# Attention maxima turned whole and split behind the transposes; eight decay products by GpSimd, one more bank copy by ScalarE

## The reference

```python
# mixer (a state space block, four heads of 64, chunks; here one chunk product per tile of 128 rows)
h = layernorm(x); z, xs, Bc, Cc, dt = split(h @ W_in)      # silu, softplus, rope
M = (Ck @ Bk.T)[None] * exp(segsum(dt * A))                # scores times decays, causal
y = M @ (xs * dt) + carried state + D * xs
x1 = layernorm(x + rms(y * silu(z)) @ W_out)
# cross attention, 16 heads of 8: q from x1, k and v from the context
att = softmax(q @ k.T / sqrt(8), axis=3); x2 = layernorm(x1 + (att @ v) @ Wo.T)
# feed-forward: each of 2048 rows goes to its best 2 of 8 experts (128 -> 512 -> 128)
out = layernorm(x2 + weighted sum of two experts)
```

## Time and profile before

| what | value |
|---|---|
| median of three runs | 432.17 us (431.09 to 432.71) |
| the profiled execution | 424.11 us, its span 422.8 us |
| mean granted clock of PE | 0.921 |
| PE busy | 343.0 us, 81% |
| DVE busy | 290.7 us, 69% |
| ACT busy | 236.0 us, 56% |
| POOL busy | 223.2 us, 53% |

### The profile page before, as it was taken

The page is one execution under the profiler, slowest core; times in us unless marked ns, Lnnn a source line. Parts: engine busy times, 40 slices in busy tenths (PEclk is TensorE's granted clock), DMA queues, the critical chain, the costliest instruction groups (busy, mean ns, idle before and its releaser), DMA issues.

```text
span 422.8 us, 8816 instructions
## 1 busy us (share of the span) xinstructions
PE 343.0 (81%) x2781; PEld 232.8 (55%) x2781; DVE 290.7 (69%) x829; ACT 236.0 (56%) x462; POOL 223.2 (53%) x322
## 2 busy tenths in 40 slices
PE   1999978888878788889877588788999999999600
PEld 1666655555534444444443344367879998998500
DVE  3465645888887898967895826356787667666455
ACT  1677645432666576544776558543545656656405
POOL 2670598854444453543589768926554333233426
PEclk9999999999998999977997669689999999999955
DMA  8833222626505040504435233301213211110163
GB/s 265 316 103 110 101 78 86 188 84 183 163 30 163 5 137 5 158 11 141 132 94 145 85 83 120 90 25 39 56 52 91 72 44 45 52 53 29 35 198 99
DMA packets 44156, 41.96 MB, mean 99 GB/s; under 512 B 4512, under 2 KB 38112, under 8 KB 44112
## 3 DMA queue, kind: packets, MB, share of 16 engines
q1 hardware_dynamic: 40976, 35.10, 28.1%
q0 software_dynamic: 2272, 4.69, 3.2%
q10 hardware_dynamic: 864, 1.61, 1.1%
HBM read 26.36 MB, written 14.75 MB: 97 GB/s over the span
## 4 chain that ended last, share of the span: by engine, by line
PE 52%; DVE 21%; POOL 13%; issue 8%; ACT 4%; DMA 3%; DVEq 0%; POOLq 0%; ACTq 0%
PE banks L993 12%; DVE nm L1186 8%; PE banks L1020 6%; POOL slots_dram L1679 4%; PE banks L690 4%; PE banks L1008 4%; PE banks L838 4%; PE banks L886 3%; PE banks L1021 2%; PE banks L747 2%; DVE ctx_in L1128 2%; ACT probs_all L1495 1%; PE banks L913 1%; POOL w_split L1691 1%; DMA ctx_in<-in_L_ffn_w 1%
## 5 line engine op out<-in xcount | busy, mean ns | idle before, releaser
L1186 DVE TENSOR_REDUCE nm<-banks 128x4 f32<-128x1024 f32 x64 | 78.0, 1219 | 16.9 <-PE banks L829 16.5
L1495 ACT ACTIVATE probs_all<-banks 128x1024 f32<-128x1024 f32 x64 | 65.4, 1022 | 39.3 <-PE banks L838 38.9
L1695 POOL DMA_INDIRECT y_dram<-x,scatter_u x39 | 37.5, 962 | 56.1 <-DVE x L1347 54.2
L993 PE MATMUL banks<-w_split,scores_in 128*128 x234 | 65.3, 415 | 0.0
L838 PE MATMUL banks<-scores_in 32*128 32x256 f32 x256 | 35.2, 352 | 24.6 <-DVE nm L1186 13.1
L838 PEld LDWEIGHTS banks<-scores_in 32*128 32x128 f32 x256 | 21.6, 202 | 50.9 <-DVE nm L1186 22.5
L1326 DVE TENSOR_TENSOR ctx_in<-ctx_in,banks 128x512 f32<-128x512 f32 x39 | 26.8, 688 | 28.6 <-ACT ctx_in L1542 28.3
L993 PEld LDWEIGHTS banks<-w_split,scores_in 128*128 128x128 f32 x234 | 41.5, 192 | 7.8 <-issue 0.8
L1679 POOL DMA_INDIRECT slots_dram<-rows,place_u x32 | 31.8, 995 | 26.3 <-DVE count L1286 18.9
L886 PE MATMUL banks<-probs_all,vals 128*9 128x256 f32 x512 | 45.1, 429 | 0.3
L1542 ACT ACTIVATE ctx_in<-banks 128x512 f32<-128x512 f32 x39 | 23.3, 598 | 36.6 <-PE banks L993 36.6
(11 more groups left out here) (222 smaller groups left out, 761.4 us busy)
## 6 DMA issues: line engine op xcount, KB each, us to landing
scores_in<-k_dram SPq DMA_DIRECT2D x32, 128.0 KB, 2.7
scores_in<-q_dram SPq DMA_DIRECT2D x32, 128.0 KB, 2.9
ctx_in<-in_L_ffn_w SPq DMA_DIRECT2D x16, 256.0 KB, 2.7
cs_wide<-cs_dram SPq DMA_DIRECT2D x14, 256.0 KB, 3.5
scores_in<-slots_dram SPq DMA_DIRECT2D x39, 65.0 KB, 1.9
k_dram<-split_qk SPq DMA_DIRECT2D x8, 256.0 KB, 2.5
q_dram<-split_qk SPq DMA_DIRECT2D x8, 256.0 KB, 2.3
ctx_in<-in_L_ffn_wo SPq DMA_DIRECT2D x8, 256.0 KB, 2.8
```

Of the source, the lines that this page charges most:

```text
L993: m = TE.matmul(up_bank(i, j), xT[:, i % XT, xh, :], all_weights[:, c + j * FF:][:, bass.ds(expert_at[i], FF)], start=n == 0, stop=n == 2)
L1186: V.tensor_reduce(most, maxima_of(n).rearrange("p (j k q) -> p j k q", j=2, k=TPS), AX_X, ALU.max, negate=True).then_inc(s["nmax"], 1)
L1495: C.activation(probs(n).rearrange("p j k q -> p (j k q)"), EXPS, ACT.Exp, scale=SCALE).then_inc(s["probs"], 1)
L1695: G.indirect_dma_start(y_dram[:, :], bass.IndirectOffsetOnAxis(ap=scatter_u[:, i:i + 1], axis=0), y_slot[:, i % Y_RING, :], None).then_inc ...
```

## The change

The maxima of a batch are transposed whole (16 columns instead of 32), in the same step as before. ACT writes the rounded part of the turned rows out of the bank (L1490, now 16 x 256), and in the step after, ahead of that step's scores, DVE writes the remainder, bank minus rounded part (`maxima_low`, 16 x 256). MISC is free only after this. SP then sends each of the two by a DMA of its own (`send_maxima`), also placed at the head of that step, and so behind the earlier step's `load_weights`. DVE's two instructions L1193 and L1195 and the tile `nm_parts` are gone. DVE's L1202 is done by ACT, as the second half of its `evacuate`. DVE's L1128 is done by POOL for the tiles from 8 on.

```diff
-SPLIT_LAG, ROWS_LAG = 0, 3
+ROWS_LAG = 3
+MATRIX_BY_POOL = 8
@@ middle_order
+        for b in range(B):
+            if n == PAIRS_B * (b + 1) - LEAD + ROWS_LAG:
+                yield "maxima_low", b
+                yield "send_maxima", b
         if exps is not None or maxima is not None:
             yield "scores", exps, maxima
...
-        for stage, lag in (("split_maxima", SPLIT_LAG), ("maxima_out", ROWS_LAG)):
-            b, late = divmod(n + LEAD + 1 - lag, PAIRS_B)
-            if not late and 1 <= b <= B:
-                yield stage, b - 1
+        for b in range(B):
+            if n == PAIRS_B * (b + 1) - LEAD - 1 + ROWS_LAG:
+                yield "maxima_out", b
@@ SP
-            def maxima_out(b):
+            def send_maxima(b):
                 r = b % RING
-                q.wait_ge(s["nm_out"], b + 1)
+                q.wait_ge(s["nm_lo"], b + 1)
                 q.wait_ge(s["nmax"], PAIRS_B * (b + 1))
-                SY.dma_start(queries[3:P:16, r, :, :].bitcast(F32), nm_rows[:, :].bitcast(F32)).then_inc(a[f"mr{r}"], 16)
+                for i in range(2):
+                    SY.dma_start(queries[3 + 16 * i:P:32, r, :, :].bitcast(F32),
+                                 nm_rows[:, i, :].bitcast(F32)).then_inc(a[f"mr{r}"], 16)
@@ PE
             def maxima_out(b):
-                q.wait_ge(s["nm_split"], 2 * (b + 1))
+                q.wait_ge(s["nmax"], PAIRS_B * (b + 1))
                 misc.wait()
                 for k in range(TPS):
-                    m = TE.transpose(MISC[0:2 * AH, k * P:(k + 1) * P],
-                                     nm_parts[:, k].rearrange("p j i r -> p (j i r)").bitcast(F32), ident)
+                    m = TE.transpose(MISC[0:AH, k * P:(k + 1) * P], nm[:, b % 2, k, :], ident)
                 m.then_inc(s["nm_t"], 1)
-                misc.freed_at(s["nm_out"], b + 1)
+                misc.freed_at(s["nm_lo"], b + 1)
@@ DVE
             def mix_matrix(t):
...
+                if t >= MATRIX_BY_POOL:
+                    return
...
-            def split_maxima(b):
...
-            def evacuate(b, half):
...
+            def maxima_low(b):
+                q.wait_ge(s["nm_hi"], b + 1)
+                V.tensor_tensor(nm_rows[:, 1, :], MISC[0:AH, 0:S], nm_rows[:, 0, :].bitcast(F32), ALU.subtract).then_inc(s["nm_lo"], 1)
@@ ACT
-                C.activation(nm_rows[:, :], MISC[0:2 * AH, 0:S], ACT.Identity).then_inc(s["nm_out"], 1)
+                C.activation(nm_rows[:, 0, :], MISC[0:AH, 0:S], ACT.Identity).then_inc(s["nm_hi"], 1)
...
             def evacuate(b, half):
+                q.wait_ge(s["av_mm"], GR * b + (half + 1) * GR // 2)
+                q.wait_ge(s["heads_t"], TPS * b)
+                q.wait_ge(a["init_dram"], INIT)
+                C.activation(avT[:, half * BANK:(half + 1) * BANK], AV, ACT.Identity).then_inc(s["av_hi" if half else "av_lo"], 1)
@@ POOL
+            def mix_matrix(t):
+                if t < MATRIX_BY_POOL:
+                    return
+                q.wait_ge(s["score"], GROUP)
+                q.wait_ge(s["decay"], t + 1)
+                G.tensor_tensor(decay[:, t % 3], decay[:, t % 3], scores[:, t, :].unsqueeze(1).to_broadcast([P, NH, P]),
+                                ALU.mult).then_inc(s["mat"], 1)
```

More of the change, by code:

```diff
@@ L371, in build @@
         nm = sb("nm", [P, 2, TPS, AH])
-        nm_parts = sb("nm_parts", [P, TPS, GJ, 2, GR], F32R)
-        nm_rows = sb("nm_rows", [2 * AH, S], F32R)
+        nm_rows = sb("nm_rows", [AH, 2, S], F32R)
         rec = sb("rec", [P, AH])
@@ L503, in build @@
         INIT = 16 * 3
-        MAX_ROWS = 16
+        MAX_ROWS = 16 * 2
         def sums_turned(t):
@@ L654, in sync_program @@
             stages = dict(keys_values=keys_values, query=query, load_keys=load_keys, load_queries=load_queries,
-                          maxima_out=maxima_out, load_weights=load_weights, sums=sums, load_sums=load_sums,
+                          send_maxima=send_maxima, load_weights=load_weights, sums=sums, load_sums=load_sums,
                           clear_rows=clear_rows, load_tile=load_tile)
@@ L1184, in maxima @@
                 q.wait_ge(s["max_mm"], n + 1)
-                q.wait_ge(s["nm_split"], 2 * (b - 1))
+                q.wait_ge(s["nm_t"], b - 1)
                 V.tensor_reduce(most, maxima_of(n).rearrange("p (j k q) -> p j k q", j=2, k=TPS), AX_X, ALU.max,
                                 negate=True).then_inc(s["nmax"], 1)
-            def split_maxima(b):
[L1190 to L1195, removed]
-            def evacuate(b, half):
[L1198 to L1202, removed]
+            def maxima_low(b):
+                q.wait_ge(s["nm_hi"], b + 1)
+                V.tensor_tensor(nm_rows[:, 1, :], MISC[0:AH, 0:S], nm_rows[:, 0, :].bitcast(F32), ALU.subtract).then_inc(s["nm_lo"], 1)
             def divide(b, half):
@@ L1356, in vector_program @@
             middle = dict(mix_matrix=mix_matrix, mix=mix, mix_residual=mix_residual, mix_norm=mix_norm,
-                          query=query, maxima=maxima, split_maxima=split_maxima, evacuate=evacuate,
+                          query=query, maxima=maxima, maxima_low=maxima_low,
                           divide=divide, out_project=out_project, x2_norm=x2_norm, gate_top=gate_top, choose=choose,
@@ L1498, in evacuate @@
             def evacuate(b, half):
-                if half == 0:
-                    q.wait_ge(s["av_mm"], GR * b + GR // 2)
-                    q.wait_ge(s["heads_t"], TPS * b)
-                    q.wait_ge(a["init_dram"], INIT)
-                    C.activation(avT[:, 0:BANK], AV, ACT.Identity).then_inc(s["av_lo"], 1)
+                q.wait_ge(s["av_mm"], GR * b + (half + 1) * GR // 2)
+                q.wait_ge(s["heads_t"], TPS * b)
+                q.wait_ge(a["init_dram"], INIT)
+                C.activation(avT[:, half * BANK:(half + 1) * BANK], AV, ACT.Identity).then_inc(s["av_hi" if half else "av_lo"], 1)
             def turn_heads(b):
@@ L1714, in pool_program @@
                 G.tensor_scalar(w_out[:, c, :], w_out[:, c, :], rms_w[:, c:c + 1], 0.5 * float(np.sqrt(DI)), ALU.mult, ALU.mult).then_inc(s["consts_g"], 1)
-            middle = dict(mask_decays=mask_decays, scale_inputs=scale_inputs, mix=mix, turn_mixed=turn_mixed,
+            middle = dict(mask_decays=mask_decays, mix_matrix=mix_matrix, scale_inputs=scale_inputs, mix=mix, turn_mixed=turn_mixed,
                           mix_residual=mix_residual, evacuate=evacuate, out_project=out_project, choose=choose, place_chosen=place_chosen,
```

2 lines of the change are left out of this document (1 added, 1 removed).

## The result

The changed kernel takes 438.41 us in the median (435.00 to 445.58, 4 runs), the kernel before beside it 432.10 (431.09 to 432.71): the record gives a ratio of 1.0248, 95% interval 1.0166 to 1.0331. The forecast was 428.5 (424.5 to 434.3). Two later comparisons gave 1.0137 (1.0041 to 1.0232) and 1.0124 (1.0086 to 1.0161). The 1.0248 is more than the listed times yield, whose medians give 1.0146, so I rely on the two repeats: the change costs about 1 to 1.5%, some 4 to 6 us.

What follows compares the result with a forecast made beforehand. PE and DVE alternate from 96 to 238 us, neither full; later a 4.1 us wait is on the path. Terms -4.1 -1.9 +1.2 -0.2 +0.6 -1.0 +1.7 sum to -3.7 us: 428.5 us, range 424.5 to 434.3.

Steps and rivals of the forecast that it cites:

- The stall: DVE's rounding copy L1193 of batch 7, 4.92 us beside POOL's run, holds up PE; removing it gives -4.1 us.
- no change: Rival: the stall is rarer in timed runs, or POOL's pieces absorb the gain; 432 us, chance 0.20.
- The maxima: Two small DVE instructions gone, -1.0 us; the new remainder ahead of reductions in batches 0 to 3, +1.7 us.
- The serial link: Rival: ACT's copy, DVE's remainder, then reduction and MISC's release in series; 1.43 us a late batch, 435.4 us, chance 0.15.
- Decay products: Eight of sixteen products move from DVE to POOL: -1.9 us on DVE, +1.2 us for normalisations waiting beside POOL.
- the 1.3 to 1.9 that was named: Sign of being right: two L1171 normalisations of batches 3 to 5 take between 1.3 and 1.9 us together.
- The copy: Second bank copy moves from DVE to ACT: -0.2 us on DVE, +0.6 us at step 49, where PE awaits ACT's exponentials.
- The clock: Rival: a shorter pause keeps PE at 2.4 GHz from 238 to 276 us; 3.5 us more gain, 425 us, chance 0.12.
- Stretch 96 to 238 within 1.5 us: Sign of being right: the stretch from 96 to 238 us stays within 1.5 us of its old length.

Runs made afterwards that it cites:

- c0: The kernel before, unaltered, profiled and timed again beside itself: ratio 0.9954 (0.9908 to 1.0001).
- e1: The kernel before with the maxima part only; second bank copy and all decay products stay on DVE: ratio 1.0115 (1.0036 to 1.0195) to before.
- g3: Maxima part alone, bank freed by ACT's unrounded copy, both rows made by DVE from SBUF: ratio 1.0116 (1.0052 to 1.0180) to before.
- g2: Maxima part alone, with DVE making each remainder twice: ratio 1.0226 (1.0131 to 1.0321) to before.
- f2: The kernel before with only the decay products of tiles 8 to 15 moved to POOL: ratio 0.9947 (0.9906 to 0.9988) to before.
- h4: The kernel before with only the decay products of tiles 8 to 15 on POOL, measured again: ratio 1.0023 (0.9978 to 1.0068) to before.
- e3: The changed kernel with all sixteen decay products given back to DVE: ratio 1.0188 (1.0106 to 1.0271) to before.
- f1: The kernel before with only the second bank copy moved to ACT: ratio 0.9973 (0.9937 to 1.0009) to before.
- f3: The changed kernel with ACT copying the bank unrounded and POOL making both rows, no remainder on DVE: ratio 1.0119 (1.0074 to 1.0165) to before.

## Why the prediction was wrong, step by step

- **The stall, -4.1 us: the step that failed.** It was taken as part of the kernel, from one execution in which seven of eight instances were 181 ns. Six further traces of kernels with this instruction have none. The text named this as the "no change" rival and argued against it by the fixed place of the instruction; the place was fixed and the meeting still was not. By the traces its worth is 0 in six of seven; the timed runs do not single it out.
- **The maxima, -1.0 and +1.7: mis-sized.** The part measures +1.15% (0.36 to 1.95), 4.9 us. The two instructions removed gave 0.45 us once (the distance at step 34, 2.34 us in c0 and 1.89 in e1); at steps 18 and 26 the 0.3 us that they gave was taken back one step later, and elsewhere DVE was idle. The remainder's 0.41 us and its place, behind L1171 in batches 0 to 3, were right, and 0.33 us a batch is what it inserts. What was not priced is the clock, about half of the loss by the estimate above, and the other half is not fully assigned. With the stall at 0 and the maxima at 4.9 in place of 0.7 the sum becomes +4.6 us, near the 4 to 6 measured.
- **The serial link** was the rival on the right side, 435.4. It had the place and the wrong partner: DVE waited for ACT in two batches only (2.6 us), and in batches 0 to 3 the remainder waited behind DVE's own normalisations. Its second half, the bank's release, was in part right: g3 shows that it is not the whole cost, and g2 beside g3 that a late release goes with 1.1%. Its remark that the rows would land at 230.1 to 231.1 against a use at 230.43 was near: the wait came at the last batch, and not in every trace.
- **Decay products, -0.7 in sum:** f2 and h4 give 0.9947 and 1.0023, so between -2.2 and +1.0 us; the term is within that. The product takes 1.28 us on POOL and not the 1.07 of the earlier trace rows, and the pair L1177 of batch 3 takes 2.17 us, outside the 1.3 to 1.9 that was named:

```profile
101.42 2.17 DVE L1177 TENSOR_SCALAR x<-r,mv,rs 128x128 f32<-128x128 f32 x2
```

  By the Trainium skill, "GPSIMD Engine Reference", section "Specifications", DVE contends with POOL in the 2-port mode or with two SBUF inputs; the trace agrees, from 1.33 us to 2.17 when POOL has the product ahead, and 404 to 412 ns for all eight remainders, which read a bank. With the products back on DVE (e3) the pair takes 1.33 us. Whether it is the mode or the inputs is not shown here.
- **The copy, +0.4 in sum:** f1 gives 0.9973 (0.9937 to 1.0009). Not contradicted; with the maxima part in place PE does wait for it (L890, 0.8 us), and e3 beside e1 leaves room for more.
- **The clock** was a rival that could only give. It took, an estimated 2.3 to 2.8 us.
- **"Stretch 96 to 238 within 1.5 us"** failed: step 48 begins 7.6 us later. It was the sign that the loss is there and not at the old stall.

## What to carry to other kernels

Before building a forecast on one long instance of an instruction, look at its other instances and at a second trace: a stall seen once in eight is not to be counted until it repeats. When a small instruction is added, ask first at which point of its engine's order it stands, and try the other points; 0.4 us of work, with the release and the sending that hang on it, cost over 1% at the head of the next step and nothing measurable in its own. Then check a theory against every variant's row: here the step that the theory blamed was longest in the variant that lost nothing. Compare the clock of whole stretches, not only the waits, and check what one trace says of the clock against the clocks of the timed runs; here they halved it.

## What the runs showed of the hardware that was not expected

**Comparisons differ by waits that have no releaser.** The kernel before took 422 us in three comparisons and 430 to 435 in the others, while its first profiled execution took 424.11. The record has the same chip number for comparisons at 422 and at 430.5 us, so the chip alone doesn't explain it. The changed kernel's first trace has such waits on ACT:

```profile
210.30 1.02 ACT L1490 ACTIVATE probs_all<-banks 128x1024 f32<-128x1024 f32 x1 [2.36 <-remote]
326.00 0.60 ACT L1536 ACTIVATE ctx_in<-banks 128x512 f32<-128x512 f32 x1 [4.33 <-remote]
```

And so has h4, which has nothing of the maxima part, in a comparison at 430.5 us:

```profile
207.03 1.02 ACT L1498 ACTIVATE probs_all<-banks 128x1024 f32<-128x1024 f32 x1 [2.84 <-remote]
326.88 0.60 ACT L1545 ACTIVATE ctx_in<-banks 128x512 f32<-128x512 f32 x1 [4.36 <-remote]
```

In the traces of the 422 us comparisons and the first one of the kernel before, the distance at step 34 is 1.9 to 2.6 us, in the seven others 3.8 to 4.3, whatever the kernel. These waits are not the change's, though in a comparison of only the first two traces they look like it. What causes them is open.

**A small row on POOL is dear.** The subtraction of 16 x 256 takes 0.72 us there and its rounding copy 0.39 (f3), where DVE needs 0.41 for the subtraction and 0.27 for the copy (g3).
